# The experts' tiles of a decoder in two sorted stages of 17 and 22 instead of three of 9, 8 and 22

## The reference

```python
def _moe(h, gate_w, w1, w2):
    t = h.reshape(B * S, D)
    logits = t @ gate_w
    top_v, top_i = jax.lax.top_k(logits, TOP_K)      # 2 of 8 experts
    gates = jax.nn.softmax(top_v, axis=-1)
    combine = jnp.zeros((T, N_EXP), t.dtype).at[jnp.arange(T)[:, None], top_i].add(gates)
    hid = jax.nn.silu(jnp.einsum('td,edh->teh', t, w1))
    ye = jnp.einsum('teh,ehd->ted', hid, w2)
    return jnp.einsum('te,ted->td', combine, ye).reshape(B, S, D)
x = x + _mla(_rmsnorm(x, g1), ...)                   # causal attention from a latent
x = x + _moe(_rmsnorm(x, g2), gate_w, w1, w2)
```

## Time and profile before

| | us |
|---|---|
| three runs | 1499.15, 1500.71, 1503.45 |
| median | 1500.71 |
| profiled execution, its time | 1513.73 |
| profiled execution, its span | 1511.9 |
| PE busy in the span | 1377.0 (91%) |
| DVE, ACT, POOL busy | 1084.0, 784.1, 152.7 |

### The profile page before, as it was taken

The page is one execution under the profiler, slowest core; times in us unless marked ns, Lnnn a source line. Parts: engine busy times, 40 slices in busy tenths (PEclk is TensorE's granted clock), DMA queues, the critical chain, the costliest instruction groups (busy, mean ns, idle before and its releaser), DMA issues. The chain is left out here.

```text
span 1511.9 us, 29598 instructions
## 1 busy us (share of the span) xinstructions
PE 1377.0 (91%) x9534; PEld 770.9 (51%) x9570; DVE 1084.0 (72%) x2571; ACT 784.1 (52%) x1491; POOL 152.7 (10%) x175
## 2 busy tenths in 40 slices
PE   6778899999999999999999999999999988889980
PEld 3456576664463544343343443344545545688970
DVE  4786654468564777799999899998868877352217
ACT  5375745536648666655455455555656535323320
POOL 1101011100100100010010000000000021233221
PEclk8899999999999999999999999999999989899995
DMA  6223313301412622442223244122223221776644
GB/s 227 78 69 106 106 37 87 100 10 41 128 33 54 181 83 70 117 122 80 86 100 86 81 146 137 44 83 68 63 67 82 52 83 55 252 255 203 213 146 154
DMA packets 124483, 158.12 MB, mean 105 GB/s; under 512 B 31372, under 2 KB 103948, under 8 KB 122348
## 3 DMA queue, kind: packets, MB, share of 16 engines
q1 hardware_dynamic: 120930, 146.88, 33.3%
q0 software_dynamic: 3408, 9.34, 1.6%
HBM read 66.34 MB, written 29.27 MB: 63 GB/s over the span
## 5 line engine op out<-in xcount | busy, mean ns | idle before, releaser
L1667 ACT ACTIVATE prob<-ps 128x512 f32<-128x512 f32 (+3 forms) x832 | 404.4, 550 | 206.0 <-PE ps L1440 108.3
L1950 DVE TENSOR_REDUCE mx<-ps 128x1 f32<-128x512 f32 (+3 forms) x512 | 281.3, 585 | 82.8 <-PE ps L1408 42.2
L1440 PE MATMUL ps<-of_expert 99*128 99x512 bf16 (+4 forms) x768 | 251.7, 356 | 12.3 <-DMA of_expert<-mrow 4.9
L1440 PEld LDWEIGHTS ps<-of_expert 99*128 99x128 bf16 (+1 forms) x768 | 73.2, 98 | 98.7 <-ACT prob L1667 37.1
L1475 PE MATMUL ps<-prob,va 128*32 128x512 f32 (+3 forms) x1024 | 115.9, 526 | 0.5 <-issue 0.4
L1406 PE MATMUL ps<-of_expert 120*128 120x512 bf16 x256 | 92.1, 380 | 3.3 <-issue 0.3
L1400 PE MATMUL ps<-of_expert 96*128 96x512 bf16 x256 | 86.8, 381 | 6.0 <-DVE mx L1946 5.0
L1946 DVE CUSTOM_DVE_ANT_0 ps<-ps,room_a 128x512 f32<-128x512 f32 x128 | 86.1, 709 | 5.4 <-PE ps L1400 5.1
L1946 DVE CUSTOM_DVE_ANT_0 ps<-ps,room_b 128x512 f32<-128x512 f32 x128 | 86.0, 710 | 1.7 <-PE ps L1400 1.4
L1657 ACT ACTIVATE mrow<-ps 12x512 bf16<-12x512 bf16 x64 | 37.3, 582 | 83.4 <-PE ps L1422 83.3
L1397 PE MATMUL ps<-of_expert 96*128 96x128 bf16 (+3 forms) x256 | 72.9, 309 | 6.8 <-DVE mx L1950 4.1
(11 more groups left out here) (243 smaller groups left out, 2558.0 us busy)
## 6 DMA issues: line engine op xcount, KB each, us to landing
of_expert<-parts SPq DMA_DIRECT2D x384, 128.0 KB, 2.4
sorted<-y SPq DMA_DIRECT2D x27, 645.0 KB, 7.6
room_a<-in_w SPq DMA_DIRECT2D x30, 512.0 KB
otc<-oraw SPq DMA_DIRECT2D x256, 32.0 KB, 1.9
room_b<-in_w SPq DMA_DIRECT2D x15, 512.0 KB
ct<-in_c SPq DMA_DIRECT2D x8, 512.0 KB, 3.5
of_expert<-in_w SPq DMA_DIRECT2D x8, 512.0 KB
wa<-in_attention SPq DMA_DIRECT2D x4, 768.0 KB, 4.6
```

The lines of the kernel that those rows point to most:

```text
L1440: i = pe.matmul(dst[:, lo:S], ks[0:rows, h, t], qs[0:rows, h, lo:S], start=(a != MASKED), stop=(a != CAUSAL and not fixed))
L1667: act.activation(prob[:, quad % PROBS, n, lo:S], key_bank(*st)[:, lo:S], ACT.Exp).then_inc(s_exp, 1)
L1950: i = dve.tensor_reduce(mx[:, slot, s, n:n + 1], src[:, 0:width], AX.X, ALU.max)
```

## The change

The sequences are grouped as (0, 1, 2) and (3), so there are two placements RB, two stages of 17 and 22 tiles, and two sets of turn semaphores, the first with one step in flight as before. No step of the attention or of a tile is added or removed; the 39 tiles, 16 SX steps and 8 loads of kept weights remain. The table of lags is replaced by another, found for this grouping. Of the lags of the causal layer and what follows it, C goes from -13.9 and -4.6 to -13.2 and -5.2 (both are added), OP's own from 2.1 to 2.3; S, P, T, V, R, N, QK, SL, OU, RS, RZ, HT, RK, RB and SX 0 stay.

```diff
-BATCHES = ((0, 1), (2,), (3,))
+BATCHES = ((0, 1, 2), (3,))
-SORTS = (1, 2, 2)
+SORTS = (1, 2)
-LAG = {"IN": 0.3, "CA": 26.5, ("CA", 0): -11.5, ("CA", 1): 8.9, "FS": 8.0, "FZ": 35.3, "SO": 15.8, "OP": -5.3, ("OP", 0): 1.6,
-       ("OP", 1): -3.9, ("OP", 3): 2.1, "M": -0.3, ("M", 1): 0.4, ("M", 2): -0.9, "C": -13.9, ("C", 0): -0.2, ("V", 1): 0.2, ("C",
-       1): 6.2, ("V", 2): -0.2, ("C", 3): -4.6, "R": -0.8, ("R", 0): -0.5, ("R", 2): -0.2, "N": -2.4, ("N", 0): 1.3, ("N", 1):
...
-       -0.5, ("EW", 0): -1.7, ("EW", 1): -27.6, "EX": 2.1, ("EX", 0): -27.6, ("EX", 1): -1.7, "QK": -3.4, ("QK", 0): 3.8, "SL":
...
-       0.9, ("EH", 2): 5.3, ("C", 2): 9.4, ("SX", 2): 2.0, ("CG", 2): 1.8, "EI": 0.5, ("CL", 1): 1.6, "RC": -11.2, ("CG", 1):
+LAG = {"IN": -0.7, "CA": 26.5, ("CA", 0): -9.5, ("CA", 1): 8.9, "FS": 8.0, "FZ": 35.1, "SO": 15.3, "OP": -5.3, ("OP", 0): 1.5,
+       ("OP", 1): -3.9, ("OP", 3): 2.3, "M": -0.3, ("M", 1): 0.4, ("M", 2): -0.9, "C": -13.2, ("C", 0): 8.3, ("V", 1): 0.2, ("C",
+       1): 2.6, ("V", 2): -0.2, ("C", 3): -5.2, "R": -0.8, ("R", 0): -0.5, ("R", 2): -0.2, "N": -2.4, ("N", 0): 1.3, ("N", 1):
...
+       -0.8, ("EW", 0): 0.1, ("EW", 1): -45.5, "EX": 2.1, ("EX", 0): -27.6, ("EX", 1): -1.7, "QK": -3.4, ("QK", 0): 3.8, "SL":
...
+       ("SX", 2): -2.1, ("CG", 2): 1.8, "EI": 0.5, ("CL", 1): 1.6, ("CG", 1): 21.5, "RK": -2.5, ("EU", 2): -0.3, "WO": -25.6,
+       ("E", 0): 0.9, ("P", 2): 3.5, "EW": -6.9, ("EW", 2): 2.8, "SX": -0.1, ("TR", 2): 0.4, "SG": -0.4, "RB": -1.8, ("EI", 0):
+       -0.4, "ML": 0.4, "XB": 0.4, ("SX", 1): -1.8}
```

## The result

The changed kernel takes **1562.11 us** (median of 4 runs, 1559.41 to 1568.06); the kernel before, run beside it on the same chip, 1502.08 (1499.15 to 1510.2). The ratio is 1.0386, 95% interval 1.0358 to 1.0414: slower by 3.9%, some 60 us. The forecast was 1537.6 with a range of 1514 to 1560. The direction was right, and so was the main path (placement, twelve sort steps, then the tiles); one of its links failed, and the time is 24.5 us above the forecast and 2 above the range. Two single executions further down (1987.46 us at a granted clock of 0.65, with both cures at once, and 1529.16 us, for the kernel before with its order worked out anew) ran apart from the others of their kernels and are left out of the medians and ratios given there.

What follows compares the result with a forecast made beforehand. The first expert tile's start and the 39 tiles' length decide: router 1265.3, first scatter 1278.0, sorted 1340.2, first tile 1350.2, tiles end 1504.9 against 1468.0. Adding 36.9 to the median 1500.7 gave 1537.6 us, range 1514 to 1560.

Steps and rivals of the forecast that it cites:

- The first tile decides: Expert tiles at the end: their start and undisturbed length set the time; first tile at 1350.2, 63.6 us later.
- 1. Work removed: One placement fewer on VectorE: sequence 2's reciprocals and router 12.9 us sooner, router ending at 1265.3 instead of 1278.24.
- as quick as sequence 1: Bound on sequence 2's router: 37.1 us from last value product to RK's end, giving 1257.4.
- rival B: Shorter links: router at 1257.4, scatters at 4.72 us, weight load issued first; 1523 us, chance 0.20.
- 2. First scatter: Placement waits for sequences 0, 1 and 2: 2.1 us to RB, 10.6 to the scatter, at 1278.0.
- 3. Twelve sort steps: First-stage scatters, one step in flight: eleven steps of 5.15 us and a 5.5 landing, 62.2 us, sorted at 1340.2.
- the kernel before covered its eight steps: First-stage sort before the change: all eight steps hidden because TensorE had sequence 3's attention beside them.
- rival C: Longer links: sequence 3's norm step holds scatters (+11.4) or sequence 2's reciprocals stay (+12.9); both 1562 us; chance 0.14.
- 4 and 5: Sorted to first up product 10 us; then 39 undisturbed tiles in 154.7 us, ending at 1504.9, +36.9.
- The tail: Collecting and last norm after the tiles: 43.9 us, untouched by the change.
- The last step, from span to median: Profiled execution stood 13.0 us above the median; the difference of 36.9 was added to the median 1500.7.

Runs made afterwards that it cites:

- both cures at once: Changed kernel with sequence 2's chain at lag -5 and four first-stage sort steps in flight, order worked out anew: 1532.03 us, ratio 1.0194.
- its order worked out anew: Kernel before with four first-stage sort steps in flight and the order of all queues replanned for it: 1507.39 us, ratio 1.0023.
- grouping alone: Kernel before with the two new stages of 17 and 22 tiles but its old table of lags: 1560.18 us, ratio 1.038.
- four in flight: Changed kernel with four semaphores of stage 0 in place of one, the written order held: 1539.65 us, ratio 1.0231.
- chain first: Changed kernel with lag -5 for sequence 2's last normalization, output products, norm, router and placement, putting them at the order's head: 1544.31 us, ratio 1.0265.
- four, norm step behind: Changed kernel with four first-stage sort steps in flight and sequence 3's norm step behind all twelve in GpSimd's queue: 1539.33 us, ratio 1.0236.
- dosed: Changed kernel with three small GpSimd power operations ahead of each first-stage sort step: 1596.92 us; the same dose in the kernel before: 1516.15 us.
- chain first without the normalization: Changed kernel with lag -5 for sequence 2's output products, norm, router and placement, its last normalization left in place: 1548.48 us, ratio 1.0295.
- the new lags alone: Kernel before, three stages kept, with the lag table of the change: 1514.3 us, ratio 1.006.
- second profile: Kernel before, unedited, profiled once more: 1505.1 us with a span of 1503.3.

## Why the prediction was right or wrong

The first tile decides, as the forecast said. Seven of the eight kernels with two stages show it: from the first up product to the end of the last piece they took 156.1 (after), 152.7 (grouping alone), 155.2 (four in flight), 156.4 (chain first), 156.6 (four, norm step behind), 156.2 (dosed) and 155.1 us (chain first without the normalization), wherever between 1335.8 and 1395.2 they began. The forecast was 154.7. The eighth, with both cures, started its tiles at 1313.7 and took 172.6, since attention was not done by then: the stretch is that short only where the tiles start late enough.

**1. Work removed: the step that failed.** The forecast's words: "I take all of it, as each link was waiting for the one before it." The 12.9 us can be followed through the links. SyncE issued the reciprocals 9.4 us sooner (1235.56 for 1244.98). The normalization ended 8.2 sooner (1244.21; before, 1252.40). The output product started 1.35 sooner (1253.55 for 1254.90). The router ended 3.6 sooner (1274.67 for 1278.24), since the links from the product on took 21.1 us for 23.3. So the forecast's 1265.3 was 9.4 us too early: 3.5 of the 12.9 were missing already at the reciprocals, 1.2 more at the normalization, and 6.8 were lost in front of the output product, of which the links behind it gave 2.2 back. It followed one chain of data and asked only whether each link waits for the one before it; one link, the output product, also waits for its place in TensorE's queue, which was full. In the kernel before the two were nearly equal, 2.5 us apart, so no wait was to be seen: what shows up when a wait goes is the next one. When the product was given the place behind its input, it followed within 0.1 us, in both kernels that were tried so with one step in flight, and the first scatter fell to 1268.8 and 1280.0. The bound "as quick as sequence 1" (RK at 1257.4) was reached by the chain-first kernel: 1257.8. The time that rival B needed was there, but not in the order that the change brought. Why the reciprocals came 9.4 us sooner isn't shown: the forecast gave it to the placement that went, but the new lags alone, with that placement still there, brought the normalization just as far forward (1243.78 for 1244.21), and the grouping alone further (1234.74), so the order that the plan found is a rival, and the edits did not part the two.

**2. First scatter.** 13.6 us from the router's end, for 12.7 forecast: TensorE's counts, which RB waits for, came 3.2 us behind it and not 2.1; from RB's start to the scatter it took 10.4 us, for 10.6.

**3. Twelve sort steps.** Right in the sum, 62.7 us for 62.2, and in that all of it is on the path: of the dose, the 33.2 us that reached the last step are in the span. The sum itself was right by luck: the first two steps took 7.8 us each and the later ones 4.8, where 5.15 was said for all, with 5.54 as the most. The first two ran beside the loads of the kept weights (DMA share 0.94 and 0.93 from the second issue to the landing), which the forecast put in idle time at no cost; no run moves these loads, so the 6 us are not shown to be theirs. That the kernel before covered its eight steps was wrong, as its dose shows. The hold of rival C did not come; it came, at 9.1 us, only where the scatters were made quicker. Its total of 1562 for two holds was met by another cause: the reciprocals did not stay where they were.

**4 and 5.** 11.0 us for 10, the weight load taking 4.83 us for 3.42; tiles 156.1 for 154.7. The tail stayed.

**The last step, from span to median,** failed too: "I add the difference to the median". The sum was 36.9 us against an execution that stood 13.0 above the median. Some 9 of these were the two stalls within the 181.4 us that the sum replaced by a clean stretch. Against the second profile (span 1503.3) the same forecast of the changed kernel's own events, a span of 1548.8, is +45.5 and not +36.9. With 1.8 us around the span it says 1550.6 us. Had the sum been tied to what it puts in and not to what it takes out, the range, moved up by the same 13.0 us, would have held the time.

What stays open: what "remote" stands for in the two stalls, and how often they come. They were seen in one of two profiles of the kernel before, and in none of the other kernels' profiles between 1280 and 1420 us.

The comparison that explains the loss as a whole is the second profile of before against after: tiles start 74.9 us later (1362.01 for 1287.12) and take 16.3 less (156.1 for 172.4), together 58.6, the difference of the spans. Two stages put the sort of 12 steps and the chain of sequence 2 on the path, and give back only what attention had cost the tiles.

## What to carry to other kernels

When a wait is removed, follow the chain with each engine's queue beside it: at every link ask what the consumer's engine has in front of it at the new time, above all on the engine that is full. Put a changed stretch in place of the old one as absolute times, and look whether the profile's own excess over the median lies inside the stretch that is replaced; a second profile of the unchanged kernel settles that. Work that is merged into one large step is paid in full as soon as no other work is left to cover it. A dose on that step, before and after, tests this, but read in the trace how much of the dose reaches the step's end: here about half of it went into a wait that the engine had anyway, which is not the same as being covered by other work.

## What the runs showed of the hardware

- A pair of scatters mostly landed later beside other transfers. From the second issue to the landing, ten of the twelve steps of the kernel after took 2.5 to 3.1 us (DMA share 0.24 to 0.30) and the first two 5.0 and 5.6 (share 0.94 and 0.93). In the chain-first kernel two steps took 6.5 and 4.9 us at shares of 0.97 and 0.79. It isn't the whole story: the first step of the kernel before landed after some 3.5 us at a share of 0.88, and steps of 4.3 us stand at 0.24 (the 4.27 of the earlier trace rows; 3.49 for the same step in the second profile) and 0.28 (chain-first). The 2.3 us that the forecast worked out from the Trainium skill ("DMA: Bandwidth & Descriptors", the anatomy of one DMA) is an estimate close to the quiet landings, and the 4.27 that it was set against was a slow one. A quiet step is 1.27 us to the second issue, 2.5 to 3.1 to the landing, and 0.73 of issue behind it.
- Scatters without a wait between them go 1.27 us apart (0.96 and 0.30): four sort steps in flight take 2.53 us each, not 4.8 or more.
- With TensorE idle from about 1323 us the granted clock was 0.50 between 1330 and 1350 us, and the forty fillers and two transposes just ahead of the first tile (4.73 us busy of five) ran at 0.55. It was 0.79 from 1360 to 1365, 0.52 from 1365 to 1370 and 1.00 from 1370 to 1375 us: the first eight us of tiles ran mostly at the lower level.
